# Scores and maximum products of layers 2 and 3 from float32r halves, and another order of work in an attention slot

## The chip, the cores and the metric

The kernel runs on one core of a Trainium2 chip. The metric is the time of one execution on the device in microseconds (us). Before the change three runs took 3499.72, 3492.97 and 3493.28 us, median 3493.28 us.

## The reference, cut to what matters

Four samples of 1024 tokens with 256 features pass through four layers. Layer 0 is a transformer block with rotary self-attention under a mask, cross-attention to 77 context tokens and an MLP. Layer 1 is a mixture of three experts. Layer 2 is again a block with self-attention (16 heads of 16 features, no mask), cross-attention and MLP, and layer 3 is one more cross-attention; the kernel works on these two together. Everything is float32. The self-attention of layer 2, which the change is about, is

```python
q, k, v = split(ln(x) @ W_qkv + b_qkv)          # 16 heads of 16 features
s = einsum('bqhd,bkhd->bhqk', q, k) * 0.25      # 1024 x 1024 for each head
o = einsum('bhqk,bkhd->bqhd', softmax(s), v)
```

The kernel computes exp(0.25 (s - max s)) with the true maximum of each query's row, and takes the sum for the division out of the product with V, where V has a column of ones.

## The kernel before, in words

`Region` (line 258) describes one attention region: `FEWR` for layer 0 and `L2R` for layers 2 and 3. A sample's 16 heads form 4 groups of 4 heads (j = 0 to 3). The heads of a group lie at partitions 32j to 32j+31, 16 rows for the head's features and others for the maximum. QE and KE hold Q and K of a whole sample in this layout, in SBUF.

A *block* is one group and one half of the queries (512). It has 8 *slots*, one for each tile of 128 keys, so a sample has 64 slots and the region 256. In a slot t, TensorE does, in the method `slot` of `region_pe`:

- four score products of slot t, one for each head: K tile (32 x 128) stationary, Q (32 x 512) moving. ScalarE takes the exponential of each (line 1896) into PB;
- four maximum products, for the block that comes 10 slots later (`lead = per + 2`): Q tile stationary, K half (512) moving. VectorE takes the maximum of each row (line 1565);
- four products of the exponentials of slot t-1 with V (`pv`), into the PSUM bank ACC.

The order is: scores 0 and 1, maximum products 2 and 3, `pv` of t-1, scores 2 and 3, maximum products 0 and 1. Products on partitions 32j with different j lie in different row groups of TensorE. All of them, and all other results of TensorE in the region, go through seven PSUM banks in a ring (`take`, `done`): the entry n waits until entry n-7 has been freed by the engine that reads it. After the last maximum product of a block, its maxima are turned by four transposes (an entry `nm`), and VectorE adds them into the rows of QE that are kept for them (line 1586), so that the score product comes out with the maximum subtracted. After the last `pv` of a block its result is turned (`tail`) and divided.

Everything else of the region is made of tokens: `lnA`, `lnB`, `lnT` (layer norm), `qk` (one 128 x 512 piece of Q or K), `v`, `oT`, `oP` (output projections), `cq`, `cm`, `cn`, `cs`, `cp`, `ct` (cross-attention), `m1`, `m2` (MLP). `overlapped` (line 526) lists the order of slots and tokens for all engines before the kernel is built. It puts tokens of the sample before and of the sample after between the slots, at most some 3.4 us of planned time (`share`) behind each slot, by the costs in `cost` and the delays in `needs`. Each engine goes through this list in order. A `qk` piece is spread by ScalarE (first half) or VectorE (second half) with two instructions into QE or KE, and in the list it waits until the sample before no longer needs these places.

## Time and profile before

| | |
|---|---|
| median of three runs | 3493.28 us |
| the profiled execution, its span | 3493.6 us |
| PE busy | 3288.6 us, 94% |
| DVE busy | 1845.4 us, 53% |
| ACT busy | 1443.6 us, 41% |
| POOL busy | 243.4 us, 7% |

PE is TensorE's matmul, PEld its weight load, DVE is VectorE, ACT ScalarE, POOL GpSimd, SP the engine that issues DMAs. Layers 2 and 3 take the span from about 1640 us to its end. Two warnings: float32 products are recorded as two instructions each ("x8" is four products), and where TensorE's products overlap or wait in pairs, its busy time is modelled and hides short waits.

### The profile page before, as it was taken

How to read it: one execution, taken by the hardware profiler on the slowest of the kernel's cores; microseconds unless marked ns; L12 is line 12 of the kernel's file. 1: busy time of each engine (PE TensorE's matmuls, PEld its weight loads, DVE VectorE, ACT ScalarE, POOL GpSimd, SP SyncE). 2: the span in 40 equal slices, each digit the busy share in tenths (PEclk: the TensorE clock that was granted, in tenths of full speed). 3: DMA queues.
4: the chain of work that ended last, by engine and by line, in shares of the span. 5: the costliest groups of instructions: out<-in, count | busy, mean ns of one | idle time of the engine just before them, and what ended most of it. 6: DMA issues, size and time to landing. Idle time of an engine off the chain costs nothing.

```text
span 3493.6 us, 49096 instructions
## 1 busy us (share of the span) xinstructions
PE 3288.6 (94%) x19540; PEld 1805.6 (52%) x19540; DVE 1845.4 (53%) x3843; ACT 1443.6 (41%) x2613; POOL 243.4 (7%) x214
## 2 busy tenths in 40 slices
PE   6899999999889999998999999999999999999887
PEld 3555666656565666666333344444444444453364
DVE  4776544562412232324766765567755666656343
ACT  0344444453412222221355455554555544555433
POOL 1100000100100000001000010010100101001010
PEclk9899999999889999999999999999999999999899
DMA  5200000002000000001000000000000000000000
GB/s 166 90 1 6 8 20 1 23 6 95 16 22 1 0 1 0 1 1 56 1 1 1 1 7 1 4 25 7 7 1 4 22 10 7 1 10 19 7 1 13
DMA packets 57256, 57.99 MB, mean 17 GB/s; under 512 B 17728, under 2 KB 51248, under 8 KB 56764
## 3 DMA queue, kind: packets, MB, share of 16 engines
q1 hardware_dynamic: 57028, 54.79, 5.0%
q8 instruction: 163, 2.67, 0.3%
q14 instruction: 65, 0.53, 0.0%
HBM read 46.89 MB, written 7.89 MB: 16 GB/s over the span
## 4 chain that ended last, share of the span: by engine, by line
PE 88%; DVE 9%; ACT 2%; issue 1%; POOL 0%; DMA 0%; DVEq 0%; SPq 0%; ACTq 0%
PE ps L902 81%; PE ps L1076 3%; DVE max_halves L1565 1%; DVE row_max_cross L1718 1%; PE ps L1203 1%; PE ps L1056 1%; PE ps L1067 1%; DVE big L1590 1%; ACT probs L1944 1%; DVE bn_stats L1619 1%; PE ps L1181 0%; ACT big L1896 0%; DVE bn_stats L1596 0%; DVE xn_tok L1632 0%; DVE big L1724 0%
## 5 line engine op out<-in xcount | busy, mean ns | idle before, releaser
L1896 ACT ACTIVATE big<-ps 128x512 f32<-128x512 f32 x1280 | 687.4, 597 | 826.7 <-PE ps L902 825.9
L902 PE MATMUL ps<-big 32*128 32x512 f32 (+2 forms) x5760 | 940.8, 603 | 16.4 <-DVE row_max L1562 4.3
L1565 DVE TENSOR_REDUCE max_halves<-ps 128x1 f32<-128x512 f32 x1024 | 652.6, 684 | 341.4 <-PE ps L902 340.0
L902 PEld LDWEIGHTS ps<-big 32*128 32x128 f32 (+1 forms) x5760 | 380.8, 188 | 494.5 <-issue 389.6
L902 PE MATMUL ps<-big,probs 128*32 128x512 f32 (+1 forms) x2688 | 379.3, 606 | 8.2 <-ACT big L1896 4.1
L902 PE MATMUL ps<-weights_mlp,big 128*128 128x256 f32 (+1 forms) x1248 | 333.0, 418 | 2.5 <-ACT big L1956 2.5
L902 PEld LDWEIGHTS ps<-weights_mlp,big 128*128 128x128 f32 x1248 | 233.7, 190 | 84.4 <-issue 58.4
L1602 DVE TENSOR_TENSOR x_tok<-ps,x_tok 128x512 f32<-128x512 f32 x112 | 77.2, 690 | 309.0 <-PE ps L902 309.0
L902 PE MATMUL ps<-x_T,weights_mlp 128*128 128x256 f32 x1024 | 231.1, 384 | 2.5 <-ACT x_T L1913 2.3
L1944 ACT ACTIVATE probs<-ps 77x512 f32<-77x512 f32 x384 | 196.1, 591 | 88.3 <-PE ps L902 88.0
L1562 DVE TENSOR_REDUCE row_max<-ps 128x2 f32<-128x512 f32 x256 | 164.6, 684 | 99.7 <-PE ps L902 99.5
L902 PEld LDWEIGHTS ps<-x_T,weights_mlp 128*128 128x128 f32 x1024 | 195.1, 193 | 36.6 <-ACT x_T L1913 5.9
L902 PEld LDWEIGHTS ps<-big,probs 128*32 128x32 f32 (+1 forms) x2688 | 75.5, 112 | 235.0 <-issue 143.4
L2091 POOL TENSOR_SCALAR eps_tile<-mean_var 128x4 f32<-128x4 f32 x56 | 13.3, 237 | 2464.2 <-DVE mean_var L1625 2464.2
L902 PE MATMUL ps<-weights,x_T 128*128 128x256 f32 x640 | 163.4, 408 | 2.9 <-ACT x_T L1871 2.9
L1718 DVE TENSOR_REDUCE row_max_cross<-ps 128x4 f32<-128x308 f32 x384 | 154.9, 470 | 13.9 <-PE ps L902 13.1
L1956 ACT ACTIVATE big<-ps,mlp_b 128x256 f32<-128x256 f32 x256 | 106.7, 470 | 130.1 <-PE ps L902 129.9
L902 PE MATMUL ps<-big,k_v_cross 32*77 32x512 f32 (+1 forms) x832 | 154.7, 627 | 2.2 <-DVE big L1724 2.2
L902 PEld LDWEIGHTS ps<-weights,x_T 128*128 128x128 f32 x640 | 126.4, 204 | 37.2 <-issue 14.6
L902 PE MATMUL ps<-weights,big 128*128 128x256 f32 x640 | 145.5, 380 | 0.0
L1833 DVE SCALAR_TENSOR_TENSOR probs<-ps,o_T,probs 128x256 f32<-128x256 f32 x96 | 46.4, 484 | 178.5 <-PE ps L902 178.5
L2006 ACT ACTIVATE big<-ps,o_T 128x512 f32<-128x512 f32 x96 | 66.0, 687 | 177.6 <-PE ps L902 177.6
(223 smaller groups left out, 3385.2 us busy)
## 6 DMA issues: line engine op xcount, KB each, us to landing
weights_mlp<-in_L_xcond_mlp_W SPq DMA_DIRECT2D x5, 1024.0 KB, 5.3
weights_mlp<-in_L_xcond_W_mlp SPq DMA_DIRECT2D x5, 1024.0 KB, 5.3
x_tok<-in_x SPq DMA_DIRECT2D x4, 1024.0 KB, 9.4
out_y<-x_tok SPq DMA_DIRECT2D x8, 512.0 KB, 2.9
big<-in_L_xcond_e_w SPq DMA_DIRECT2D x3, 1024.0 KB, 10.1
gates_biases<-mod_rows SPq DMA_DIRECT2D x20, 128.0 KB, 5.0
big<-in_L_xcond_adaLN_W SPq DMA_DIRECT2D x1, 2304.0 KB
kc_groups<-x_tok SPq DMA_DIRECT2D x3, 616.0 KB, 8.4
```

The lines of the kernel that those rows point to most:

```text
L902: return pe.matmul(out, lhsT, rhs, start=first, stop=last)
L1056: last = pe.transpose(PS[:, bank, i * P:(i + 1) * P], OT[:, c:c + P], ident[:, :])
L1076: last = pe.transpose(PS[:, banks[ft], (t % 4) * P:(t % 4 + 1) * P], rows[:, t, ft * P:(ft + 1) * P], ident[:, :])
L1562: dve.tensor_reduce(NM[:, 2 * qh + e, c:c + 2], PS[:, bank, :].rearrange("p (t n) -> p t n", t=2), AX.X, ALU.max, negate=True).then_inc(R. ...
L1565: dve.tensor_reduce(NMP[:, e, j, qt, hf:hf + 1], PS[:, bank, :], AX.X, ALU.max, negate=True).then_inc(R.frees(key), 1)
L1602: dve.tensor_tensor(x, PS[:, R.bank(key), :], x, ALU.add).then_inc(R.frees(key), 1)
L1718: dve.tensor_reduce(dst, src, AX.X, ALU.max, negate=True).then_inc(R.frees(key), 1)
L1833: dve.scalar_tensor_tensor(ROU[hf][:, t, :], PS[:, M.EXPERT[o % 2], 0:D], RP[:, 4 * hf + t, e:e + 1], ROU[hf][:, t, :], ALU.mult, ALU.add) ...
L1896: act.activation(PB[:, score % 2, j, :], PS[:, R.bank(key), :], ACT.Exp, scale=SCALE).then_inc(R.frees(key), 1)
L1944: act.activation(PC[0:NC, j, :], PS[0:NC, R.bank(key), :], ACT.Exp, scale=SCALE).then_inc(R.frees(key), 1)
L1956: last = act.activation(HT[hf][:, m, :], PS[:, R.bank(key), i % 2 * D:(i % 2 + 1) * D], ACT.Gelu_apprx_tanh, bias=B1[:, 0 if R.l == 0 else ...
L2006: act.activation(dst, PS[:, M.HIDDEN[q % 3], :], ACT.Silu, bias=ANC[:, m, b:b + 1]).then_inc(e_hsb, 1)
```

## The change

For `L2R` alone (`split`), Q and K are no longer kept as float32 in SBUF. ScalarE writes a piece with its bias as float32r (a "hi" half), VectorE writes what is left of it as a second float32r tile (a "lo" half). SP stores the halves to DRAM and later loads them back by block, so that 32 rows of a head hold, for K, 16 rows hi and 16 rows lo, and for Q two such tiles, (hi, lo) and (lo, hi). A product of Q and K is then two float32r products of 32 rows that add up in one bank. The score has a third, of a constant (two rows of ones) with the maxima, also as hi and lo halves (`MR`). In a slot all four scores come first, then `pv`, then all four maximum products. The maxima run 11 slots ahead; VectorE's addition into QE is replaced by a copy on ScalarE, and GpSimd splits the maxima. The core of the diff (waits for DMAs, tile and semaphore names left out):

```diff
+ROW_HI, ROW_LO = 0, 4
+Q_BLOCKS, K_GROUPS, STAGES = 3, 2, 2
...
+        QR = within_big("q_blocks", [P, Q_BLOCKS, 2, HALF], 0)
+        KR = within_big("k_groups", [P, K_GROUPS, SEQ], 3072)
+        STG = within_big("qk_parts", [P, STAGES, 2, HALF], 5120)
+        MR = within_big("max_rows", [P, 2, HALF], 7168)
...
-                self.lead = self.per + 2
+                self.split = l == 2
+                self.lead = self.per + (3 if self.split else 2)
...
+                    if self.split:
+                        return shown[0] + shown[1] + self.fills(fill, 0) + self.fills(fill, 1) + [("tail", q) for q in tails] + [("nm", q) for q in nms]
...
+            if R.split:
+                return out + [("qk", b, m, a, hf) for m in range(KT) for a, hf in ((1, 0), (1, 1), (0, 0), (0, 1))] + [("v", b, m) for m in range(KT)]
...
+            if kind == "slot" and R.split:
+                return (1.9 if tok[1] is not None else 0.0) + (0.95 if tok[2] is not None else 0.0) + 0.45 * len(tok[4]) + 0.45 * len(tok[5])
...
+                if kind == "qk" and R.split:
+                    return True
...
+            def block_fits(n):
+
+                b, g, qh = R.block(n)
+                parts = [("qk", b, g // 2, 0, qh)] + ([("qk", b, g // 2, 1, hf) for hf in range(NH)] if qh == 0 else [])
+                return all(k in ended for k in parts) and (n < Q_BLOCKS or state["t"] > (n - Q_BLOCKS + 1) * R.per)
...
+                    if tok[0] == "qk" and R.split:
...
+                        sp.wait_ge(*R.freed(tok))
+                        for x, part in enumerate((0, 1) if a else (0, 1, 0)):
+                            dst = KPd[b, m, :, x, :, hf * HALF:(hf + 1) * HALF] if a else QPd[b, m, hf, :, x]
+                            sp.dma_start(dst, STG[:, n % STAGES, part, :].bitcast(F32)).then_inc(R.part_out[n % STAGES], 16)
+                    if tok[0] == "ld":
...
+                        if n >= Q_BLOCKS:
+                            sp.wait_ge(R.pv, (n - Q_BLOCKS + 1) * R.per)
+                        if qh == 0:
...
+                            sp.dma_start(KR[:, u, :].bitcast(F32), KPd[b, m].rearrange("(j e) x r n -> e j (x r) n", e=2)[e]).then_inc(R.kg_in[u], 16)
...
+                        for x in range(2):
+                            sp.dma_start(QR[:, n % Q_BLOCKS, x, :].bitcast(F32), ...)
...
+                def by_parts(t, f):
+                    keys, stationary, moving = [], [], []
+                    if t is not None:
...
+                        if i == 0:
+                            pe.wait_ge(*R.freed(("nm", n)))
+                        for j in range(HG):
+                            rows = slice(32 * j, 32 * j + 32)
+                            keys.append(("sc", t, j))
+                            stationary.append([KR[rows, u, kt * P:(kt + 1) * P]] * 2 + [SUB[rows, :]])
+                            moving.append([QR[rows, n % Q_BLOCKS, 0, :], QR[rows, n % Q_BLOCKS, 1, :], MR[rows, n % 2, :]])
+                    for key in R.fills(f, 0) + R.fills(f, 1):
...
+                        keys.append(key)
+                        stationary.append([QR[rows, n % Q_BLOCKS, x, c:c + P] for x in range(2)])
+                        moving.append([KR[rows, u, hf * HALF:(hf + 1) * HALF]] * 2)
+                    banks = []
+                    for step in range(3):
+                        for i, key in enumerate(keys):
+                            if step == 0:
+                                banks.append(take(key))
+                            if step < len(moving[i]):
+                                last = mm(PS[:, banks[i], :], stationary[i][step], moving[i][step], step == 0, step == len(moving[i]) - 1)
+                                if step == len(moving[i]) - 1:
+                                    done(last, key)
+
                 def slot(tok):
                     _, score, fills, product, tails, nms = tok
-                    for half in range(2):
+                    if R.split:
+                        by_parts(score, None)
+                        if product is not None:
+                            pv(product)
+                        by_parts(None, fills)
+                    for half in range(0 if R.split else 2):
...
+                        elif R.split:
...
+                            dve.wait_ge(R.part_hi, n + 1)
+                            dve.scalar_tensor_tensor(parts[:, 1, :], PS[:, R.bank(tok), 0:w], QB[:, 3 * a, m:m + 1], parts[:, 0, :].bitcast(F32), ALU.add, ALU.subtract).then_inc(R.frees(tok), 1)
...
+                    for n in nms if R.split else ():
...
+                        copy(MR[:, n % 2, :], PS[:, R.bank(("nm", n)), :]).then_inc(R.frees(("nm", n)), 1)
...
+                        elif R.split:
...
+                            if n >= STAGES:
+                                act.wait_ge(*R.parts_landed(*R.parted[n - STAGES]))
+                            act.activation(STG[:, n % STAGES, 0, :], PS[:, R.bank(tok), 0:w], ACT.Identity, bias=QB[:, 3 * a, m:m + 1]).then_inc(R.part_hi, 1)
...
+                    for n in tok[5] if kind == "slot" and R.split else ():
+                        pool.wait_ge(R.nm_f, n + 1)
...
+                        pool.tensor_copy(halves[:, :, ROW_HI:ROW_HI + 4].bitcast(F32R), NMF[:, n % 2]).then_inc(R.nm_h, 1)
+                        pool.wait_ge(R.nm_h, n + 1)
+                        pool.tensor_tensor(halves[:, :, ROW_LO:ROW_LO + 4], NMF[:, n % 2], halves[:, :, ROW_HI:ROW_HI + 4], ALU.subtract).then_inc(R.nm, 1)
```

## Rows read from the trace of the kernel before

**Rows 1.** The page: busy time of each engine; the chain that ended last.

```profile
PE 3288.6 (94%) x19540; PEld 1805.6 (52%) x19540; DVE 1845.4 (53%) x3843; ACT 1443.6 (41%) x2613; POOL 243.4 (7%) x214
PE 88%; DVE 9%; ACT 2%; issue 1%; POOL 0%; DMA 0%; DVEq 0%; SPq 0%; ACTq 0%
```

**Rows 2.** Stretches: start:end length, busy of PE, PEld, DVE, ACT, POOL, clock, DMA.

```profile
1700.00:1930.00 230.00, 229.04 (x1436) 76.40 (x1436) 152.22 (x255) 122.86 (x233) 0.00 (x0) 1.00 0.00 1
1975.00:3288.00 1313.00, 1270.39 (x8196) 584.66 (x8188) 801.29 (x1568) 680.52 (x1242) 104.99 (x77) 0.97 0.03 9
```

**Rows 3.** Groups by shape, 1640 to 3493 us: busy, mean ns | idle before, releasers.

```profile
L902 PE MATMUL ps<-big 32*128 32x512 f32 x4096 | 719.5, 650 | 5.8 <-DVE max_halves L1565 4.0 <-DVE row_max_cross L1718 1.1 <-DVE big L1724 0.6
L1565 DVE TENSOR_REDUCE max_halves<-ps 128x1 f32<-128x512 f32 x1024 | 652.6, 684 | 341.4 <-PE ps L902 340.0
```

**Rows 4.** Timeline, slots between tokens (start, length, engine, line, what).

```profile
2607.62 1.06 PE L902 MATMUL ps<-big,probs 128*32 128x512 f32 x8
2608.61 1.14 PE L902 MATMUL ps<-big 32*128 32x512 f32 x8
2609.68 0.66 PE L1056 MATMUL ps<-ident,o_T 128*128 128x128 f32 x4
```

**Rows 5.** Timeline, two slots that follow each other directly.

```profile
1788.94 1.06 PE L902 MATMUL ps<-big,probs 128*32 128x512 f32 x8
1789.93 2.93 PE L902 MATMUL ps<-big 32*128 32x512 f32 x16
1790.90 0.20 PEld L902 LDWEIGHTS ps<-big 32*128 32x128 f32 x3 [0.22 <-issue]
1791.09 2.06 ACT L1896 ACTIVATE big<-ps 128x512 f32<-128x512 f32 x4 [1.54 <-PE ps L902]
1791.18 2.48 DVE L1565 TENSOR_REDUCE max_halves<-ps 128x1 f32<-128x512 f32 x4 [1.20 <-PE ps L902]
1791.74 0.29 PEld L902 LDWEIGHTS ps<-big 32*128 32x128 f32 x2 [0.64 <-ACT big L1896]
1792.79 1.06 PE L902 MATMUL ps<-big,probs 128*32 128x512 f32 x8
```

**Rows 6.** Timeline, 16-bit and 8-bit products of 512 columns, in the preparation.

```profile
81.85 1.03 PE L902 MATMUL ps<-probs,ones_b 128*128 128x512 fp8e4 x4
```

**Rows 7.** The same products, by tile: min, median, max of one in ns.

```profile
L902 PE MATMUL ps<-probs,ones_b x16: 379/620/634, 77.3 to 82.5; 128*128 128x512 fp8e4 x16
```

**Rows 8.** Timeline, a cross-attention maximum product, four row groups.

```profile
2071.35 0.60 PEld L902 LDWEIGHTS ps<-k_v_cross,x_T 32*128 32x128 f32 x16 [0.66 <-issue]
2071.38 0.81 PE L902 MATMUL ps<-k_v_cross,x_T 32*128 32x154 f32 x16 [0.45 <-DVE row_max_cross L1718]
2071.98 0.77 PE L902 MATMUL ps<-big 32*128 32x512 f32 x2
```

**Rows 9.** Who waited for whom, 1975 to 3288 us: total us, times, longest.

```profile
PEld ps L902 <- DVE max_halves L1565: 40.3, 56, 4.1
PEld ps L902 <- ACT big L1896: 35.6, 54, 1.6
```

**Rows 10.** Timeline, the start of layer 2.

```profile
1645.72 3.81 PE L902 MATMUL ps<-weights,probs 128*128 128x128 f32 x32 [1.00 <-DVE probs L1637]
1649.37 7.03 PE L902 MATMUL ps<-probs,weights 128*128 128x512 f32 x16
1659.90 1.14 PE L902 MATMUL ps<-big 32*128 32x512 f32 x8
```

**Rows 11.** DMA issues: count, KB each, median us from issue to landing.

```profile
weights<-in_L_xcond_W_proj SPq DMA_DIRECT2D x4, 256.0 KB, 3.0
```

**Rows 12.** Groups by shape on DVE, ACT and POOL that the change replaces or meets.

```profile
L1586 DVE SCALAR_TENSOR_TENSOR big<-ps,group_cols,big 128x512 f32<-128x512 f32 x32 | 23.7, 742 | 2.4 <-PE ps L1067 2.4
L1871 ACT ACTIVATE o_T<-ps 128x512 f32<-128x512 f32 x32 | 19.4, 607 | 0.3 <-PE ps L902 0.3
L2066 POOL TENSOR_TENSOR weights_mlp<-weights_mlp,gates_biases 128x2048 f32<-128x2048 f32 x4 | 18.1, 4536 | 2.2 <-DMA gates_biases<-mod_rows 2.2
```

91 lines of the change are left out of this document (81 added, 10 removed).

## The prediction

> **What bounds the kernel now.** I read the shares of the engines first: PE is busy for 94% of the span and carries 88% of the chain of waits, DVE 53%, ACT 41% [rows 1]. So time is to be had from PE, but the share of a whole span says nothing of one stage. By stretches, layers 2 and 3 have two kinds. From 1700 to 1930 us the first sample's slots run almost alone; 1436 matmul records at 24 per slot are at most 60 slots, some 56 after the transposes are taken off. From 1975 to 3288 us about 190 slots run with tokens between them, PE busy 97%, DVE 61%, ACT 52% [rows 2]. I count 60 slots of the first kind and 196 of the second, 256 in all.
>
> A slot between tokens costs PE 0.99 us for `pv` and 1.07 us for each set of four products of 32 rows, so 3.13 us [rows 4]. A slot without tokens should cost less (its two sets stand side by side), but takes 3.85 us: the 16 records of 1789.93 stretch over 2.86 us, with a product that starts only at 1791.74, released by an exponential [rows 5]. There the ring of banks is the limit, not the array. This wait is not seen in PE's busy time. It is seen by division: 4096 records are 512 sets and were "busy" 719.5 us, 1.41 us each, where a clean one takes 1.07 [rows 3, 4]. Some 170 us are waits, about 56 in the 60 bare slots (0.93 each) and 115 in the others. The waits that the profile names end on VectorE's reductions and ScalarE's exponentials [rows 9].
>
> **The products.** Before there is no float32r product in the trace. What it does show: a product of 8-bit and 16-bit operands with 512 columns comes each (1.03 - 0.379)/3 = 0.217 us [rows 6, 7]. A float32 product is two records, and a set of four in different row groups takes 1.07 = 4 x 0.217 + 0.20, that is, each float32 product streams its columns four times, the row groups beside each other, and 0.20 us is the first weight load and the drain before another shape [rows 4, 6]. For a float32r product the bounds are one stream (0.217, by the 16-bit rows) and four (0.87, by the float32 rows). I take one: four streams are what the halves of two float32 operands need (hi hi, hi lo, lo hi, lo lo), and a float32r operand is written here as one such half, so it is nearer to the 16-bit rows. Then the scores of a slot cost 3 x 0.217 + 0.20 = 0.85, the maximum products 2 x 0.217 + 0.20 = 0.63, the slot 0.85 + 0.99 + 0.63 = 2.47 us against 3.13, a saving of 0.66. At two streams it is 1.50 + 0.99 + 1.07 = 3.56, a loss of 0.43; at four, 5.6.
>
> More weight loads: 20 for each slot where 8 products had 16. Each row group must load 128 columns for every 0.217 us of streaming. The cross maximum products do it faster: 16 records in four row groups pass in 0.60 us, four after each other in 0.15, their loads beside them [rows 8]. So I cost the loads at nothing; if each were bare at about 0.1 us (half of the 0.20 above), three steps would lose 0.3 per slot, and the saving would be 0.35. The number of changes between 32-row and 128-row products stays: two sets and one `pv` before and after.
>
> **Bare slots.** Let the reductions of slot t begin at M. The ring has 7 entries, a slot 8: the fourth score of t+1 needs the bank of the first maximum of t, free at M + 0.68 + 0.05 = 0.73 [rows 3, 5]. It loads and streams to 1.48 (0.10 + 0.65), drain to 1.58, `pv` to 2.57, maximum products to 3.10, and the reduction sees them 0.28 later (first set over at 1790.90, VectorE starts 1791.18) [rows 5]: 3.38. The other loop, the third maximum product of t+1 behind the last reduction of t (2.48 + 0.05 = 2.53), just fits under 2.57. Period 3.38 for 3.85, so 0.47 x 60 = 28 us. With bare loads the period is 0.3 longer, and it is 0.17 x 60 = 10.
>
> **Slots between tokens.** Free of waits they give 0.66 x 196 = 129 us. But the reductions (0.60 each, four in 2.48 [rows 5]) are no longer two in the middle and two at the end: all four begin at the end of the slot, and what comes next on VectorE, a token's reduction or addition, comes 1.2 us later than before. Queued behind them are that token's banks, and then the ring. Where a long token follows, nothing is lost; where a short cross-attention step follows, PE waits. I take a quarter of the slots: 196 x 0.25 x 1.2 = 59 us. Bounds: none, and half (118). Net 70 us.
>
> The Trainium skill has a rule against this change (TensorEngine Tiling (Array Packing), PSUM Bottleneck): tiling speeds up TensorE but not the emptying of PSUM, which may become the bottleneck. By it the bare slots would be held by the reductions alone, and the slots between tokens might give nothing; it is the third rival below.
>
> **Pieces and staging.** The 32 `qk` pieces lose two spreading instructions and gain one each on ScalarE and VectorE, no more than before. New is the way through DRAM. A store of 256 KB should land in about 3.0 us [rows 11], a load as well. With two stages, ScalarE waits for the store of the piece before the last. In later samples a piece costs PE about 1.9 us (half of 3.81 [rows 10]) and slots lie between, so I take 0.2 us for each, 6 us; bounds 0 and 2 us each (64), if pieces come in pairs and ScalarE, with the exponentials queued behind it, stands. At the start, before, the first maximum product comes at 1659.90, after the products for V (7.03 us at 1649.37) [rows 10]. After, the pieces come first: K done by about 1651, first Q stored by about 1656, loaded by 1659 to 1662, with the V products beside it. Cost 3 us, bounds 0 and 12. Loads of later blocks wait on SP for `pv` of a block that ends five slots (over 16 us) before they are needed, against 3 us; what is queued behind them on SP are weight loads needed far later. Cost 0; if that cover went, each block would lose up to 3 us, 96 in all.
>
> **Maxima.** VectorE loses 32 additions of 0.74 us, ScalarE gains 32 copies of 0.60 [rows 12], neither on the path. GpSimd now stands in the way from maxima to transposes; it may be in a 4.5 us gating of weights [rows 12], but the maxima run one slot further ahead and there are two slots (over 5 us) until the transposes. Cost 0, bounds 0 and 4 x 4.5 = 18 us.
>
> **Sum.** 28 + 70 - 6 - 3 = 89 us. The profiled execution has a span of 3493.6 us, 0.3 above the median of the runs, so I use it as it is: 3493.6 - 89 = 3405 us.
>
> **Rivals.**
> 1. *The array's saving arrives whole* (the waits don't grow): 28 + 129 - 9 = 148, so 3345 us. For it: tokens between slots come to 1313/190 - 3.13 - 0.59 = 3.2 us, longer than four reductions. Against it: waits are there already, 0.59 us in each such slot [rows 3].
> 2. *Staging stands in ScalarE's way* (2 us for each of 32 pieces in place of 0.2): 3405 + 58 = 3463. For it: two stages only, three stores for a Q piece. Against: slots between.
> 3. *VectorE's late reductions take it all*, slower. The place is the bank that PE takes first after a slot; the price is 1.2 us; with the 28 us of the bare slots kept and 9 paid, it decides from (129 + 19)/(196 x 1.2) = 63% of the slots on. At 80%: 129 + 19 - 188 = -40, so 3534 us. For it: rows 9, and a ring that a slot fills alone. Against: VectorE has 39% idle in the stretch [rows 2].
> 4. *Two streams for a float32r product*: 196 x 0.43 = 84 lost, bare slots 0.73 + 1.40 + 0.10 + 0.99 + 0.97 + 0.28 = 4.47 for 3.85 (37), 9 paid, 3624 us. For it: each operand still has four bytes. Against: nothing in the trace.
> 5. *The row groups don't run beside each other in float32r*: 20 products of 0.217 in a row and `pv` are 5.5 us, 2.4 more for 196 slots and 1.7 more for 60, 570 us lost, about 4065. The float32 products of the same rows do run so.
>
> **Chances.** Forecast 0.45, rival 1 0.22, rival 2 0.09, rival 3 0.11 (nearly all of it over the change's 0.2%, a little at no change), rival 4 0.09, rival 5 0.04. A change of 0.2% (7 us) is what a measurement of this kernel can tell from none. Faster 0.76, within 0.2% 0.04, slower 0.20. The range leaves out rivals 4 and 5, the far end of 3 and what is beyond rival 1: 3335 to 3510 us. Among the faster cases alone I would say 3340 to 3465.
>
> **What would show it.** Right: 32-row float32r records that start 0.217 us after each other in a row group, with their loads beside them; a slot between tokens from 3.13 to about 2.5 us; bare slots at a period of 3.4; four reductions together after each slot, and more waits of PE on them; first maximum product at about 1662. Wrong: steps of 0.32 (bare loads) or 0.43 (two streams); a period of the bare slots above 3.85; ScalarE waiting for stores in front of exponentials; a lower granted clock than 1.00 in the bare slots, where PE will stand still for 0.9 of 3.4 us.

## The result, and the profile after

The changed kernel takes 3530.0 us (median of four runs, 3525.16 to 3531.72) against 3496.5 us of the kernel before, measured beside it (four runs, 3492.97 to 3500.87). The ratio is 1.009, 95% interval 1.007 to 1.0115: slower by 0.9%, where I forecast 3405 us and a range up to 3510. The profiled execution took 3529.47 us, its span is 3527.7 us, and the span before is 3493.6, so 34 us have to be found.

The page after, busy shares and chain of waits, against [rows 1]:

```profile
PE 3222.9 (91%) x20564; PEld 1885.5 (53%) x20564; DVE 1809.8 (51%) x3812; ACT 1447.1 (41%) x2645; POOL 256.7 (7%) x278
PE 78%; DVE 13%; ACT 3%; DMA 2%; issue 2%; SPq 1%; POOL 1%; DVEq 0%; ACTq 0%; POOLq 0%
```

PE is busy for 66 us less and carries ten points less of the chain; VectorE carries four more, and DMA and SP's queue appear. Work left PE, and waits came in its place. Where they stand is seen by stages. Each stage here is bounded by the same events in both traces (first layer-norm transpose of layer 2, the product with V of the first slot, of the 65th and of the last); in brackets the time within it at the lower of TensorE's two clock levels, 1.2 GHz.

| stage | before, us | after, us | difference |
|---|---|---|---|
| layers 0 and 1 (code unchanged) | 1641.1 [136] | 1648.0 [154] | +7 |
| start: to the first product with V | 60.5 [21] | 122.5 [75] | +62 |
| the first 64 slots | 274.3 [0] | 249.3 [3] | -25 |
| the other 192 slots | 1312.7 [68] | 1295.9 [140] | -17 |
| after the last product with V | 204.9 [20] | 211.8 [41] | +7 |

The same four stages of layers 2 and 3 as windows of the trace after (start:end, length, busy of PE, PEld, DVE, ACT and POOL, clock as a share of 2.4 GHz, DMA share, GB/s). The second and third lines answer to the two of [rows 2]:

```profile
1648.00:1770.00 122.00, 67.99 (x276) 39.84 (x276) 52.48 (x101) 14.59 (x22) 15.59 (x12) 0.69 0.37 121
1770.00:2020.00 250.00, 243.98 (x1976) 112.61 (x1972) 177.76 (x307) 146.68 (x281) 6.89 (x19) 0.99 0.10 35
2020.00:3315.00 1295.00, 1204.42 (x8922) 630.49 (x8916) 768.19 (x1534) 678.49 (x1261) 114.31 (x123) 0.95 0.09 30
3315.00:3527.00 212.00, 174.47 (x1061) 111.85 (x1060) 87.83 (x210) 77.70 (x140) 18.07 (x15) 0.90 0.02 6
```

In the first line no engine has much to do: PE works for 68 of 122 us, and the 16 DMA engines together are at 37%. In the third PE is busy for 93%, where it was 97% [rows 2]. A mean clock of 0.69 over 122 us is 0.31/0.5 = 62% of them at 1.2 GHz; before, the same stage ran at 0.83. In the bare slots of the second line the clock is 0.99, so the lower clock that I had named as a sign there hardly came.

**The products, by shape,** from 1640 us on (busy us, mean ns | idle before). The moving tile is named first: `k_groups,q_blocks` is a maximum product, `q_blocks,k_groups` a score, `max_rows,max_rows_ones` the score's third stream. Each float32r stream is one record. They answer to [rows 3]:

```profile
L978 PE MATMUL ps<-q_blocks,k_groups 32*128 32x512 f32 x2048 | 320.4, 479 | 10.8 <-DVE big L1854 3.0 <-DVE row_max_cross L1848 0.9 <-DVE qk_parts L1817 0.4
L978 PE MATMUL ps<-max_rows,max_rows_ones 32*128 32x512 f32 x1024 | 144.3, 407 | 0.0
L978 PE MATMUL ps<-k_groups,q_blocks 32*128 32x512 f32 x2048 | 226.1, 470 | 70.7 <-DVE qk_parts L1817 36.8 <-DMA q_blocks<-q_parts 16.5 <-ACT big L2026 7.0
L1682 DVE TENSOR_REDUCE max_halves<-ps 128x1 f32<-128x512 f32 x1024 | 634.9, 682 | 417.2 <-PE ps L978 414.8
```

Score sets and maximum sets together cost PE 691 us for 719.5 before, although a quarter of the scores' streams and half of the maxima's are gone: busy time still holds waits, as it did before. What a set costs without them is read from a slot whose banks are all free. Timeline, a slot between two tokens of the second kind of stretch, against [rows 4]:

```profile
2610.39 0.74 PE L978 MATMUL ps<-q_blocks,k_groups 32*128 32x512 f32 x8
2610.96 0.40 PE L978 MATMUL ps<-max_rows,max_rows_ones 32*128 32x512 f32 x4
2611.29 1.06 PE L978 MATMUL ps<-big,probs 128*32 128x512 f32 x8
2612.29 0.74 PE L978 MATMUL ps<-k_groups,q_blocks 32*128 32x512 f32 x8
2612.96 7.17 PE L978 MATMUL ps<-x_T,weights_mlp 128*128 128x256 f32 x32
2613.05 2.48 DVE L1682 TENSOR_REDUCE max_halves<-ps 128x1 f32<-128x512 f32 x4 [1.79 <-PE ps L978]
```

Scores 0.90, product with V 1.00, maximum products 0.67: 2.57 us for 3.13. Three streams of 0.90 and two of 0.67 differ by 0.23, so a float32r product does stream its columns once, in about 0.22 us, with its weight loads beside it and the four row groups beside each other. Now the same kind of slot ten microseconds earlier:

```profile
2599.75 0.84 ACT L2097 ACTIVATE big<-ps,mlp_b 128x256 f32<-128x256 f32 x2 [0.89 <-PE ps L978]
2600.54 1.07 PE L978 MATMUL ps<-big,probs 128*32 128x512 f32 x8
2600.68 1.28 ACT L2026 ACT_TABLE_LOAD   x1
2601.54 0.50 PE L978 MATMUL ps<-k_groups,q_blocks 32*128 32x512 f32 x3
2601.98 2.06 ACT L2026 ACTIVATE big<-ps 128x512 f32<-128x512 f32 x4
2602.63 0.73 PE L978 MATMUL ps<-k_groups,q_blocks 32*128 32x512 f32 x5 [0.59 <-ACT big L2026]
```

Three maximum products find a bank. The fourth needs the one of this slot's own first score (eight results, seven banks), and ScalarE came late to it: a token's activation, then 1.28 us of table load. The slot takes 3.65 us (2599.64 to 2603.29), with one stall for the whole set. Two slots in direct succession, against [rows 5]:

```profile
1795.74 1.06 PE L978 MATMUL ps<-big,probs 128*32 128x512 f32 x8
1796.73 0.74 PE L978 MATMUL ps<-k_groups,q_blocks 32*128 32x512 f32 x8
1797.32 1.66 PE L978 MATMUL ps<-q_blocks,k_groups 32*128 32x512 f32 x8
1797.50 2.48 DVE L1682 TENSOR_REDUCE max_halves<-ps 128x1 f32<-128x512 f32 x4 [1.51 <-PE ps L978]
1798.24 0.29 PEld L978 LDWEIGHTS ps<-q_blocks,k_groups 32*128 32x128 f32 x5 [0.26 <-DVE max_halves L1682]
1799.14 1.07 PE L978 MATMUL ps<-big,probs 128*32 128x512 f32 x8
```

The period is 1799.14 - 1795.74 = 3.40 us. The load of 1798.24 comes right behind VectorE's first reduction (1797.50 + 0.68): the fourth score waits for the bank of the first maximum, as forecast.

**The start of layer 2,** timeline, against [rows 10]. SPq lines are DMAs issued by SP:

```profile
1650.45 3.64 SPq L920 DMA_DIRECT2D gates_biases<-in_L_xcond_b_mlp  x1
1654.22 0.75 DVE L1817 SCALAR_TENSOR_TENSOR qk_parts<-ps,q_bias,qk_parts 128x512 fp32r<-128x512 f32 x1 [1.73 <-ACT qk_parts L2066]
1659.34 3.42 SPq L879 DMA_DIRECT2D k_parts<-qk_parts  x4
1666.64 0.69 ACT L2066 ACTIVATE qk_parts<-ps,q_bias 128x512 fp32r<-128x512 f32 x1 [10.82 <-DMA k_parts<-qk_parts]
1676.48 1.07 SPq L893 DMA_DIRECT2D q_blocks<-q_parts  x2
1676.54 0.69 ACT L2066 ACTIVATE qk_parts<-ps,q_bias 128x512 fp32r<-128x512 f32 x1 [6.72 <-DMA q_parts<-qk_parts]
1686.78 0.79 PE L978 MATMUL ps<-k_groups,q_blocks 32*128 32x512 f32 x2 [16.47 <-DMA q_blocks<-q_parts]
1690.57 0.69 ACT L2066 ACTIVATE qk_parts<-ps,q_bias 128x512 fp32r<-128x512 f32 x1 [13.34 <-DMA q_parts<-qk_parts]
1711.60 0.69 ACT L2066 ACTIVATE qk_parts<-ps,q_bias 128x512 fp32r<-128x512 f32 x1 [20.34 <-DMA k_parts<-qk_parts]
```

The first K piece is in its stage at 1654.97; its store is issued at 1659.34, since SP issues in order and has loads of weights, biases and cross-attention tiles before it. The third piece's copy starts at 1666.64, 7.3 us after that issue: that is the landing that I had put at 3.0 us [rows 11]. That figure was the median of four loads, issued at 1640.84, 2021.64, 2479.94 and 2907.55 us of the trace of before. Taken apart (count, KB each, median us to landing), the one at the start of layer 2 took more than twice as long as the three later ones:

```profile
weights<-in_L_xcond_W_proj SPq DMA_DIRECT2D x1, 256.0 KB, 6.6
weights<-in_L_xcond_W_proj SPq DMA_DIRECT2D x3, 256.0 KB, 2.8
```

So the trace of before already had the higher price where it was needed. In the trace after, the chain is in plain sight: 10.82, 6.72, 13.34 and 20.34 us of ScalarE in front of a stage that is still being stored. The first block of Q is issued at 1676.48, and its first maximum product is at 1686.78, where I had said 1662 (the layer itself begins 7 us later than before).

### The profile page after: what moved, and what is told of

It reads as the page before. It is cut to its first block, busy times and chain, and to the rows that moved or that the text cites. A ratio compares the mean times of both kernels' runs of the same rounds, so it can differ in the third digit from the quotient of the medians.

```text
span 3527.7 us, 51568 instructions
## 1 busy us (share of the span) xinstructions
PE 3222.9 (91%) x20564; PEld 1885.5 (53%) x20564; DVE 1809.8 (51%) x3812; ACT 1447.1 (41%) x2645; POOL 256.7 (7%) x278
## 4 chain that ended last, share of the span: by engine, by line
PE 78%; DVE 13%; ACT 3%; DMA 2%; issue 2%; SPq 1%; POOL 1%; DVEq 0%; ACTq 0%; POOLq 0%
PE ps L978 73%; DVE max_halves L1682 5%; PE ps L1191 2%; DVE row_max_cross L1848 1%; DMA k_parts<-qk_parts 1%; DMA q_parts<-qk_parts 1%; PE ps L1318 1%; ACT big L2026 1%; PE ps L1182 1%; DVE xn_tok L1754 1%; PE ps L1170 1%; ACT probs L2085 1%; SPq L879 1%; DVE big L1854 1%; DVE bn_stats L1741 1%
## 5 line engine op out<-in xcount | busy, mean ns | idle before, releaser
L2026 ACT ACTIVATE big<-ps 128x512 f32<-128x512 f32 x1280 | 666.1, 603 | 608.4 <-PE ps L978 607.4
L1682 DVE TENSOR_REDUCE max_halves<-ps 128x1 f32<-128x512 f32 x1024 | 634.9, 682 | 417.2 <-PE ps L978 414.8
L978 PE MATMUL ps<-big,probs 128*32 128x512 f32 (+1 forms) x2688 | 389.7, 623 | 2.2 <-ACT big L2026 1.0
L978 PE MATMUL ps<-q_blocks,k_groups 32*128 32x512 f32 x2048 | 320.4, 479 | 10.8 <-DVE big L1854 3.0
L978 PE MATMUL ps<-k_groups,q_blocks 32*128 32x512 f32 x2048 | 226.1, 470 | 70.7 <-DVE qk_parts L1817 36.8
L978 PEld LDWEIGHTS ps<-k_groups,q_blocks 32*128 32x128 f32 x2048 | 95.1, 194 | 309.7 <-issue 220.1
L978 PE MATMUL ps<-big 32*128 32x256 f32 (+2 forms) x1664 | 223.4, 490 | 9.9 <-DVE row_max L1679 4.3
L978 PEld LDWEIGHTS ps<-q_blocks,k_groups 32*128 32x128 f32 x2048 | 144.8, 190 | 155.0 <-issue 64.1
L978 PEld LDWEIGHTS ps<-big 32*128 32x128 f32 (+1 forms) x1664 | 141.2, 192 | 108.5 <-issue 80.4
L978 PE MATMUL ps<-big,k_v_cross 32*77 32x512 f32 (+1 forms) x832 | 173.8, 639 | 3.2 <-DVE big L1854 2.2
```

Source lines behind the costliest of these rows:

```text
L978: return pe.matmul(out, lhsT, rhs, start=first, stop=last)
L1682: dve.tensor_reduce(NMP[:, e, j, qt, hf:hf + 1], PS[:, bank, :], AX.X, ALU.max, negate=True).then_inc(R.frees(key), 1)
L2026: act.activation(PB[:, score % 2, j, :], PS[:, R.bank(key), :], ACT.Exp, scale=SCALE).then_inc(R.frees(key), 1)
```

## The experiments

Two accounts are tried: most of what was lost is the start (pieces that wait for two stages, and DMAs on few engines behind a full queue of SP), or it is the order, that is, four results in a row that VectorE alone empties. Rivals: bare weight loads or two streams, GpSimd in the way of the maxima, or a change of shape between sets. The theories in the expectations below carry letters of their own. Each ratio is to the kernel before on the same chip; its median was 3495.6 to 3498.0 us on all of them. Times are medians, the stages are those of the table above in one profiled execution of each kernel, which can lie off the median (stages_6 3482.71, halves_order 3465.07, extra_stream 3558.77, all_maxima_on_dve 3406.3).

| kernel | time, us | ratio (95%) | start | 64 slots | 192 slots |
|---|---|---|---|---|---|
| changed kernel | 3530.0 | 1.009 (1.007 to 1.0115) | 122.5 | 249.3 | 1295.9 |
| one_store | 3459.79 | 0.9895 (0.986 to 0.9929) | 74.6 | 247.2 | 1278.0 |
| stages_6 | 3491.96 | 0.9989 (0.9971 to 1.0007) | 91.6 | 249.1 | 1286.0 |
| halves_order | 3472.91 | 0.9936 (0.9914 to 0.9958) | 122.4 | 245.6 | 1237.9 |
| fp32_order | 3558.24 | 1.0186 (1.0153 to 1.0219) | 62.0 | 281.5 | 1360.4 |
| halves_stages_6 | 3438.83 | 0.9836 (0.982 to 0.9853) | 91.9 | 243.6 | 1243.2 |
| halves_stages_loads | 3430.39 | 0.9817 (0.98 to 0.9833) | 84.6 | 246.2 | 1237.1 |
| all_maxima_on_dve | 3420.87 | 0.9789 (0.976 to 0.9818) | 84.5 | 241.6 | 1219.9 |
| max_first | 3613.83 | 1.033 (1.0313 to 1.0348) | 122.7 | 309.3 | 1324.0 |
| extra_stream | 3568.23 | 1.0211 (1.0194 to 1.0228) | 122.7 | 263.2 | 1317.5 |
| ring6_new_order | 3653.3 | 1.0448 (1.0423 to 1.0473) | 123.1 | 285.8 | 1378.1 |
| ring6_mixed_sets | 3581.63 | 1.0239 (1.0216 to 1.0263) | 123.7 | 270.3 | 1323.5 |
| pv_last | 3563.94 | 1.019 (1.0166 to 1.0214) | 125.4 | 247.7 | 1320.7 |
| short_max_new_order | 3371.49 | 0.9643 (0.9626 to 0.9661) | 115.3 | 218.9 | 1176.8 |
| short_max_mixed_sets | 3444.5 | 0.9843 (0.9817 to 0.9869) | 112.6 | 243.2 | 1230.3 |

**one_store.** Only the first piece is stored, and every block and group is loaded from it; the other stores, and the waits for them, are gone. It leaves out the way of Q and K through DRAM, and keeps every product and load.

```diff
-                        for x, part in enumerate((0, 1) if a else (0, 1, 0)):
-                            sp.dma_start(dst, STG[:, n % STAGES, part, :]...)
+                        if n == 0:
+                            for part in range(2):
+                                sp.dma_start(FIXd[:, part * HALF:(part + 1) * HALF], STG[:, 0, part, :]...)
-    sp.dma_start(KR[:, u, :].bitcast(F32), KPd[b, m]...)
+    sp.dma_start(KR[:, u, :].bitcast(F32), FIXd)
```

> Leaves out the way of Q and K through DRAM: only the first piece is stored, and every block loads its Q and K tiles (same sizes) from that one store, so the attention of layer 2 works on wrong numbers. Theory A (the start of layer 2 is lost to the staging of pieces, which costs little later): the first product with V comes near 1705 us instead of 1770, the later slots take what they take now (1296 us for the last 192), about 3530 - 60 = 3470. Theory B (staging also holds ScalarE, VectorE and PE among the later slots): another 20 to 60 us in the later slots, 3410 to 3450. Theory C (the order of work and the late reductions eat the gain there): the later slots don't move.

It took 3459.79 us, 70 less than the changed kernel: 48 at the start and 18 in the 192 slots, so the time lies between those of theories A and B. Its start, 74.6 us, still has the loads of Q and K and one store, and is 14 above that of the kernel before.

**stages_6.** Pieces 2 to 5 of the first sample have a stage each, in free columns of `big`.

```diff
+        STGX = within_big("qk_parts_more", [P, 4, 2, HALF], 12288)
+        def stage(n):
+            return STGX[:, n - 2] if 2 <= n < 6 else STG[:, n % STAGES]
-                            parts = STG[:, n % STAGES]
+                            parts = stage(n)
```

> Four more staging buffers for the first sample's pieces 2 to 5, in a part of SBUF that is free then; nothing else. Theory A (two stages make each pair of pieces wait for a DMA round trip at the start): the start shortens by 30 to 50 us, 3480 to 3500. Rival (the DMAs themselves are the limit at the start, all on one queue with SP's waits in order): under 15 us, 3515 or more. The later slots stay as they are in both.

3491.96 us (ten runs): 38 us back, 31 of them at the start. Waiting for a stage is half of what the start lost.

**halves_order.** The products stay float32r; the slot order is the former one, in sets of four: two scores with two maximum products, product with V, then the other two and two.

```diff
-                        by_parts(score, None)
+                        by_parts(score, fills, 0)
                         if product is not None:
                             pv(product)
-                        by_parts(None, fills)
+                        by_parts(score, fills, 1)
...
```

> The changed kernel with the order of before in a slot: scores 0 and 1 with maximum products 2 and 3 step by step, the product with V, then scores 2 and 3 with maximum products 0 and 1. Two shapes of 32-row work in a set: 3 streams and 2. Theory C (four late reductions hurt the slots between tokens): the last 192 slots shorten by 20 us or more although PE pays 3 + 3 streams in place of 3 + 2 (0.22 us for each slot, 56 in all); total 3500 to 3520. Rival (the order is worth it, the ring is not the limit between tokens): longer by up to 56 us, 3550 to 3590; the bare slots get longer than 3.40 in any case.

3472.91 us, 57 less than the changed kernel and below the 3500 to 3520 expected, with the same start (122.4) and the same tail. The 192 slots take 58 us less, although their PE work is larger: by its timeline a set of two and two costs 0.90, so a clean slot 2.79 us for 2.57. The bare slots did not get longer, as both theories had it, but shorter (3.32 us).

**fp32_order.** The kernel before, with the new order alone.

```diff
+                    if R.l == 2:
+                        for half in range(2 if score is not None else 0):
+                            scores(score, half)
+                        if product is not None:
+                            pv(product)
+                        for key in R.fills(fills, 0) + R.fills(fills, 1):
+                            fill(key)
...
```

> The kernel before (float32 products) with the new order alone in layers 2 and 3: four scores, product with V, four maximum products. PE's own work in a slot stays 3.13 us. Theory C (late reductions): slower than before, 3510 to 3540. Rival (the order itself costs nothing or helps the ring): bare slots from 3.85 to 0.73 + 0.97 + 0.10 + 0.99 + 0.97 + 0.28 = 4.04 by the same chain of bank waits as in the prediction, 12 us, the others unchanged: 3495 to 3510.

3558.24 us, 62 above the kernel before and more than the 3510 to 3540 expected: 48 in the 192 slots, 7 in the 64. So in either arithmetic the order costs some 50 to 60 us in the 192 slots. The period of the bare slots is 3.95 us, where I had expected 4.04.

**halves_stages_6** and **halves_stages_loads.** The first is both edits together. The second also loads each block with four DMAs, one per head of 32 rows, and puts the weight loads of the first sample behind the loads of the layer's first rows on SP.

```diff
-                            sp.dma_start(KR[:, u, :].bitcast(F32), KPd[b, m].rearrange("(j e) x r n -> e j (x r) n", e=2)[e])
+                            for j in range(HG):
+                                sp.dma_start(KR[32 * j:32 * j + 32, u, :].bitcast(F32), KPd[b, m, 2 * j + e].rearrange("x r n -> (x r) n"))
```

> Order of before and six stages at the start together, both with float32r halves. If the two losses are separate terms (57 us for the order in the last 192 slots, 38 us for the stages in the stretch before the first product with V), they add: 3530 - 57 - 38 = 3435 us. If they were one (for example both through TensorE's clock), less: 3450 to 3470.

> The same, and two changes of the DMAs: each load of a block's Q or K tile is issued as four DMAs, one for each head (32 rows), and the first sample's weight loads are issued behind the first block's loads in place of before them. Theory A1 (the transfers of the first blocks run on few DMA engines and behind weight loads in one queue): the first product with V comes 10 to 20 us earlier, 3415 to 3425. Rival (after six stages nothing of the start waits on transfers, but SP issues three times as many loads, 0.5 us each): no gain, 3435 or more.

3438.83 us: 91 less than the changed kernel, where 57 and 38 add up to 95. The two costs are separate, as far as 4 us can tell. The second edit brings 8 more, 7 of them at the start, less than the 10 to 20 expected. The loads of the first block, timeline of halves_stages_6 and then of halves_stages_loads:

```profile
1667.65 1.07 SPq L902 DMA_DIRECT2D q_blocks<-q_parts  x2
1677.84 1.23 PE L987 MATMUL ps<-k_groups,q_blocks 32*128 32x512 f32 x8 [13.77 <-DMA q_blocks<-q_parts]
```

```profile
1658.08 2.41 SPq L906 DMA_DIRECT2D k_groups<-k_parts  x4
1662.92 3.55 SPq L910 DMA_DIRECT2D q_blocks<-q_parts  x8
1668.02 1.23 PE L995 MATMUL ps<-k_groups,q_blocks 32*128 32x512 f32 x8 [4.84 <-DMA q_blocks<-q_parts]
```

From the first issue of a Q load to the first maximum product it is 10.2 us in the one and 5.1 in the other, although the same bytes now take eight issues. The Trainium skill has a rule for it (DMA: Bandwidth & Descriptors, Why a DMA increments its semaphore by 16 and not by 1): a DMA is spread over the largest number of engines, up to 16, that divides the slowest dimension of both its access patterns. By that rule a block's load, with four heads as its slowest dimension, runs on 4 engines, and the loads by head on all 16. The trace agrees for the loads by block: in the changed kernel, from 1675.5 to 1678.5 us with the load of K alone in flight, and from 1684 to 1687 with that of Q, the DMA share is 0.26 and 0.27, which is 4 of 16 engines, at 103 GB/s. Of the loads by head it shows less than 16: 0.52 from 1664 to 1667 us of halves_stages_loads, where SP takes 3.55 us to issue eight of them. Over the whole start the DMA share is 0.37 in the changed kernel, 0.47 in stages_6 and 0.56 here. Windows of the last two:

```profile
1640.00:1731.00 91.00, 66.84 (x282) 39.04 (x280) 51.83 (x99) 14.80 (x23) 14.90 (x12) 0.74 0.47 159
```

```profile
1642.00:1726.00 84.00, 67.83 (x272) 40.93 (x274) 53.08 (x102) 14.70 (x22) 15.88 (x13) 0.76 0.56 175
```

The loads by head and the later weight loads weren't tried apart, so how the 7 us divide between them is open.

**max_first.** The slot turned round: four maximum products, product with V, four scores.

```diff
-                        by_parts(score, None)
+                        by_parts(None, fills)
                         if product is not None:
                             pv(product)
-                        by_parts(None, fills)
+                        by_parts(score, None)
```

> The changed kernel with a mirrored order: four maximum products first, product with V, four scores. PE's own work, streams and changes of shape are those of the changed kernel; now VectorE's reductions run beside the product with V and the scores, and ScalarE's exponentials start at the end of the slot. Theory C1 (it is the lateness of the reductions, in front of tokens that need VectorE, that costs): the last 192 slots from 1296 to 1240 to 1260 us; the bare slots get longer, to about 4.0 us, since the product with V then waits for exponentials of the slot before (60 slots x 0.6 = 36 us). Rival C2 (it is the slot of four plus four entries in a ring of seven, whichever comes first): the last 192 slots stay at 1280 or more.

3613.83 us, 84 more than the changed kernel, of which 60 are in the 64 slots and 28 in the 192. So C1's price did not come, and the 192 slots stay above 1280 as C2 has it. The bare slots go to a period of 4.27 us, from 3.40: the product with V now waits there for exponentials of the slot before (0.84 us at 1831.04, released by ScalarE), as was expected. Between the slots this order gains 27 us and in them it loses 55 (table in the next section), so late reductions were bad for the tokens, and turning the sets round costs more in the slots than it brings there.

**extra_stream.** The first stream of each score product is issued twice (256 x 0.217 = 56 us of PE).

```diff
+                                if step == 0 and key[0] == "sc":
+                                    mm(PS[:, banks[i], :], stationary[i][step], moving[i][step], True, True)
```

> The changed kernel, with the first stream of each score product issued twice (the first result is overwritten by the second), 0.22 us more of PE in each of 256 slots, 56 us in all. If PE's work still sets the time: 3586 us. If waits on VectorE and ScalarE set it, and TensorE's clock falls because PE stands still: less than 25 us slower, with fewer us at half clock in the last 192 slots than the 140 of the changed kernel.

3568.23 us, +38 for 56. Bare slots take it in full (3.40 to 3.63), the 192 slots only 22 of 42. So the array is the limit for part of the slots, and in the rest a stream fits into a wait that is there anyway. Part of the 20 us can be the clock: the time at 1.2 GHz in the 192 slots fell from 140 to 109 us. The bare slots confirm one stream of 0.22 us, and the others that the saved streams did not all arrive.

**ring6_new_order** and **ring6_mixed_sets.** The ring of banks has six entries in place of seven, in either order.

```diff
+                self.depth = 6 if self.split else 7
-                    return RING[n % 7]
+                    return RING[n % self.depth]
```

> The changed kernel with six banks in the ring of layers 2 and 3 in place of seven. Theory C2 (a set of four results that one engine empties needs more of the ring): the order with four scores and four maximum products loses more from a missing bank than the order with mixed sets; here 80 us or more over the changed kernel (bare slots about 0.6 us longer, the others too), and twice what the mixed sets lose. Rival C3 (the ring's depth isn't what counts, only when the reductions start): under 40 us, and the same in both orders.

> The kernel with float32r halves and mixed sets (3473 us) with six banks in the ring. Theory C2: it loses less than the new order does from the same bank, 20 to 60 us. Rival C3: as much as the new order.

+123 and +109 us. Neither theory's prices came: the loss is over 80 us as C2 has it, but nearly the same in both orders as C3 has it. A bank is worth 110 to 120 us in either order. The ring limits both, so its depth does not explain the difference between them.

**pv_last.** Mixed sets, both ahead of the product with V.

```diff
                         by_parts(score, fills, 0)
-                        if product is not None:
-                            pv(product)
                         by_parts(score, fills, 1)
+                        if product is not None:
+                            pv(product)
...
```

> Float32r halves, mixed sets, but both sets first and then the product with V. By the ring (8 entries of a slot in 7 banks) the last maximum product takes the bank of the slot's own first score, which is free 0.19 + 0.60 + 0.05 = 0.84 us after the first set, and now no product with V covers this: bare slots about 3.4 us, and 0.5 to 0.7 us lost in each of the other 192, so 3570 to 3610. If sets of mixed readers alone were what matters and the place of the product with V did not: 3465 to 3480.

3563.94 us, 91 more than halves_order and just under the 3570 to 3610 expected: 83 of it in the 192 slots (0.43 each, where 0.5 to 0.7 was expected; 0.60 inside the slots, and less between them), almost none in the bare ones (3.37 for 3.32). The product with V is the time in which the banks of the first set are emptied; without it between the sets, eight results come in a row.

**all_maxima_on_dve.** halves_stages_loads, with the cut of the maxima into two parts on VectorE, GpSimd out of that chain.

```diff
-                        pool.tensor_copy(halves[:, :, ROW_HI:ROW_HI + 4].bitcast(F32R), NMF[:, n % 2])
-                        pool.tensor_tensor(halves[:, :, ROW_LO:ROW_LO + 4], NMF[:, n % 2], ..., ALU.subtract)
+                                dve.tensor_copy(parts[:, :, ROW_HI:ROW_HI + 4].bitcast(F32R), NMF[:, n % 2])
+                                dve.tensor_tensor(parts[:, :, ROW_LO:ROW_LO + 4], NMF[:, n % 2], ..., ALU.subtract)
...
```

> The kernel of the run with mixed sets, six stages and loads by head (3430 us), with the maxima split into their two halves by VectorE in place of GpSimd, which may be in a long gating of weights when the maxima come. Theory D (PE's transposes of the maxima wait for GpSimd: the trace lists some 20 us of it): 3410 to 3420. Rival (two more small operations and waits on VectorE in 32 blocks cost what is won): 3428 to 3435.

3420.87 us, the fastest complete kernel: 2.1% under the kernel before and 3.1% under the changed one. Its gain of 10 us over halves_stages_loads is not shown: it was measured on another chip, the intervals of the two ratios overlap, its runs spread from 3406.3 to 3432.67, and its stages in the table are of the fastest of them. What speaks for it is a wait of the changed kernel (2020 to 3250 us; who waited for whom, us in total, times, longest), which is gone from the same stretch of all_maxima_on_dve:

```profile
PEld ps L978 <- DVE max_halves L1682: 51.5, 141, 1.6
PEld ps L978 <- ACT big L2026: 27.9, 61, 0.9
PE ps L978 <- DVE max_halves L1682: 23.7, 28, 2.3
...
PEld ps L1182 <- POOL row_max L2226: 16.0, 6, 3.8
```

The weight loads of six transposes stood up to 3.8 us for GpSimd. GpSimd's own timeline in the 192 slots has, five times, the cut of the maxima right behind a multiplication of token rows by gates (2.37 us at 2183.51, the cut at 2185.82), where I had thought of the weights.

**short_max_new_order** and **short_max_mixed_sets.** What was still open after these was why the orders differ: by the reader, or by something in PE's sequence. So VectorE reads 128 of the 512 columns of each maximum product (each reduction 284 ns for 682), in the changed kernel and in halves_order. It leaves out three quarters of the keys in the maxima. PE's work is untouched.

```diff
-    dve.tensor_reduce(NMP[...], PS[:, bank, :], AX.X, ALU.max, negate=True)
+    dve.tensor_reduce(NMP[...], PS[:, bank, 0:P] if R.split else PS[:, bank, :], AX.X, ALU.max, negate=True)
```

> The changed kernel, but in layer 2 each reduction looks at 128 of its 512 columns (the rest of the keys is left out of the maximum), so it should take about 0.3 us in place of 0.68. Theory E (a set of four results with a single reader is emptied too slowly for the ring): the order's penalty goes, so this kernel comes to within 20 us of the one with mixed sets and short reductions, or below it (PE's own work is 0.22 us less in each slot); 3400 to 3430. Rival F (the penalty is on PE's side, in the changes of shape or in the weight loads of scores with scores): it stays some 50 us above that kernel.

> The kernel with float32r halves and mixed sets, with the same short reductions. Theory E: gains less from them than the new order does, 30 to 50 us, 3425 to 3445. Rival F: gains as much as the new order.

The new order gains 159 us (more than expected), the mixed one 28, with the same 0.398 x 1024 = 408 us taken from VectorE in both. So it is not VectorE's load as such that costs, and rival F falls too: in the new order a set of four results has VectorE as its only reader, and the time of its reductions counts. With short reductions the sign turns: the new order is 73 us ahead of the mixed one. PE's saving, absent in the changed kernel, is there: the 192 slots take 1176.8 us, and the bare ones 3.06 each. The reduction, and what VectorE waits for before it, in short_max_new_order:

```profile
L1682 DVE TENSOR_REDUCE max_halves<-ps 128x1 f32<-128x128 f32 x1024 | 226.4, 284 | 525.2 <-PE ps L978 522.9
```

and in the stretches of short_max_new_order and halves_order that answer to the third window of the changed kernel:

```profile
2000.00:3165.00 1165.00, 1110.97 (x8856) 591.60 (x8856) 480.24 (x1504) 669.36 (x1250) 112.04 (x119) 0.99 0.10 33
```

```profile
2013.00:3250.00 1237.00, 1159.37 (x8922) 615.03 (x8918) 774.93 (x1533) 690.16 (x1260) 114.58 (x123) 0.97 0.10 31
```

The clock goes with the waits: 0.95 in the changed kernel, 0.97 in halves_order, 0.99 in short_max_new_order. The waits of PE in halves_order (2020 to 3250 us) show the other half of it:

```profile
PE ps L976 <- ACT big L2024: 31.9, 44, 1.3
PEld ps L976 <- ACT big L2024: 30.1, 43, 1.5
PEld ps L976 <- DVE max_halves L1680: 19.7, 34, 1.7
...
PE ps L976 <- DVE max_halves L1680: 4.1, 7, 1.5
```

The same stall can stand in a row of PE and in one of PEld, so they are not added. In PE's own rows it is 4.1 us behind reductions, for 23.7 in the changed kernel, and 31.9 behind exponentials, for 7.0: the waits have moved from VectorE to ScalarE, and their sum did not fall (36 us for 31). These rows alone therefore don't explain the 58 us. Most of it lies inside PE's modelled busy time, 1159 us here and 1204 in the changed kernel, though the work here is 42 us more; the next section divides it by place.

## Why the prediction was wrong

The forecast was 89 us faster; the profiled span is 34 us longer. The 123 us between them, by the terms of the sum (measured for 64 and 192 slots, where I had counted 60 and 196):

| term | forecast, us | measured, us | off by |
|---|---|---|---|
| start of layer 2 | -3 | -62 | 59 |
| PE's saving between tokens | 129 | 0.56 x 192 = 108 | 21 |
| staging in the slots | -6 | -18 (one_store) | 12 |
| late reductions and other waits (measured: what is left) | -59 | 17 + 18 - 108 = -73 | 14 |
| bare slots | 28 | 25 | 3 |
| tail, layers 0 and 1 | 0 | -14 | 14 |

**The step that failed is the start of layer 2,** "Cost 3 us, bounds 0 and 12". I took a median landing of 3.0 us from four weight loads and used it for each DMA of a chain of stores and loads. Three things were wrong with it. The queue of SP was not empty: the first store was issued 4.4 us after its piece was ready. The landing was 7.3 us for a K piece, which is two stores of 256 KB and not one, and 10.3 us from the issue of a Q block to its first product; of the four loads, the one in this very place had taken 6.6. And I counted one such chain: in the first sample all pieces come in a row through two stages, so the stores stand in ScalarE's way again and again. That is rival 2's mechanism, priced there for later samples (0.09), and it struck in the one place where there are no slots to hide it. At the start ScalarE stands idle for 62 us in all in front of a stage whose store ends last, and for 15 us in stages_6. one_store removes 48 of the 62 us, stages_6 removes 31. I had written the sentence "With two stages, ScalarE waits for the store of the piece before the last", and did not apply it here. With 12 us at the start in place of 62 the time would be about 3480 us, inside the range, but still 75 us above the forecast: the other 64 us of the 123 are in the terms below.

**The products were right.** The trace has one stream of 0.22 us per float32r product, the row groups beside each other and the loads hidden; rivals 4 and 5 fall by the clean slot of 2.57 us and by extra_stream. The size was off by 0.10 us a slot (2.47 forecast): I gave a set 0.20 us beside its streams, and it has 0.23 to 0.25.

**The bare slots were right,** with their mechanism: 3.40 us for 3.38, the fourth score behind the first reduction.

**The late reductions** were half of their term. What is left in the table, 73 us for 59, lies inside the bounds of 0 and 118, but it is a remainder and not a measurement of reductions. Where it lies can be read from the traces, if the stage of the 192 slots is divided into PE's time from the first product of a slot to its last, and the rest, which is tokens with the waits among them:

| kernel | in the slots, us | between them, us |
|---|---|---|
| before | 706 | 607 |
| fp32_order | 721 | 640 |
| changed kernel | 647 | 650 |
| halves_order | 635 | 605 |
| short_max_new_order | 593 | 585 |
| short_max_mixed_sets | 634 | 597 |
| max_first | 702 | 623 |
| pv_last | 750 | 572 |

The slots gained 59 of the 108 us, and the time between them grew by 42. The forecast's mechanism, a token behind late reductions, is the 42 (33 in fp32_order, none in halves_order). The other 49 were lost inside the slots, where the forecast had no waits to come: maximum products that find no bank, as behind the table load in the slot of 2599.64, and the rest of it was not taken apart. Both parts hold the 18 us that one_store gives back, and some GpSimd in front of transposes (18 us was my bound; PE stands 13 us for it, the weight loads 16).

They also hold the lower clock. The time at 1.2 GHz in these 192 slots doubled, from 68 to 140 us. The Trainium skill describes this (TensorE: Matmul & The Clock Gate, A second HAM failure mode: psum-queue depth-cycling): where TensorE stands still for a moment in each round of its PSUM banks, its clock swings between the two levels. This trace agrees in kind. What the clock alone cost here no run shows, but there is a price for an estimate. Layers 0 and 1 are the same code in all 16 traces; they took 1639.3 to 1648.0 us with 133 to 154 us at 1.2 GHz, which is 0.36 us for each us at the lower level, and the stage after the last product with V gives 0.32 in the same way (205 to 217 us, 20 to 53 of them at 1.2 GHz). At 0.36 the 72 us more would be some 26 of the 73.

What the forecast did not ask is what the order costs against the former order. It costs 58 us by halves_order, and since that order has 0.22 x 192 = 42 us more of PE work, about 100 us of waits and lower clock: 55 in the slots and 45 between them. The time at 1.2 GHz is 140 us in the one and 65 in the other, so by the estimate above some 27 of the 100 are clock. This is the larger lesson of the two, because the order is a free choice.

**Rival 3 named nearly the measured time,** 3534 us, but not for its reason. It wanted late reductions in 80% of the slots, 188 us; 73 were found (at my price of 1.2 us that is 32% of the 192 slots), and the rest came from the start. A rival that gives the right number can still be the wrong account, and only the table by stages shows it. The rule of the Trainium skill that the prediction weighed (TensorEngine Tiling (Array Packing), PSUM Bottleneck) held for the slots between tokens, where 17 of 108 us arrived; in the same section the Trainium skill advises emptying PSUM with both ScalarE and VectorE, and mixed sets let both do it at the same time.

**Open.** The tail is 7 to 12 us longer in every float32r kernel, and layers 0 and 1 are 7 us longer in the changed one, both with unchanged code. Both go with the clock: 20 to 41 us at 1.2 GHz in the tail, 136 to 154 in layers 0 and 1, which at 0.32 and 0.36 make 7 and 6 us. Why the lower clock is granted more often in the tail is open. Why mixed sets gain only 28 us from short reductions is read from waits on ScalarE, not shown by an experiment that shortens the exponentials.

## What to carry to other kernels

Before a saving on TensorE is booked, count per round of the PSUM ring how many results each reader gets in a row: seven banks with a set of four for one reader lost 58 us against sets that two readers empty side by side, although the latter cost TensorE more. A round trip through DRAM is priced where nothing covers it, at the first use, with the number of stages, the position in the issuing queue and the shape of the transfer, not by the median landing of some other load. Where two edits come together (here arithmetic and order), forecast each against the former state of the other, since one of them may be a plain loss.

## What the runs showed of the hardware

A float32r product of 512 columns and 32 rows streams in about 0.22 us, like the 8-bit and 16-bit one in [rows 6], and four row groups run beside each other with their loads hidden. The stores of a 512 KB K piece landed 7.3 us after their issue; a 256 KB weight load took 6.6 us at the start of layer 2 and 2.8 later. The same Q block needed 10.2 us as two DMAs (halves_stages_6) and 5.1 as eight, with the weight loads behind it (halves_stages_loads); the two DMAs alone in flight moved 103 GB/s at a DMA share of 0.27. Layers 0 and 1, the same code in 16 traces, were 0.36 us longer for each us that stood at 1.2 GHz. A seventh bank of the ring is worth 110 to 120 us here (ring6_new_order, ring6_mixed_sets), about as much as the products' whole saving between tokens (108).
